# A metaformer block on one core: dot products through TensorE, one centring, sums per chunk, and other loop starts

## The reference, cut to what matters

```python
x = x + _L1_conv_ref(_ln_c(x), ...)      # _ln_c: (v - mean) / sqrt(var + 1e-6) over channels

center = x[:, :, H // 2, W // 2][:, :, None, None]
sim = (x * center).sum(1, keepdims=True) / (jnp.linalg.norm(center, axis=1, keepdims=True) * jnp.linalg.norm(x, axis=1, keepdims=True) + 1e-06)
x = x * (sim >= 0.7).astype(x.dtype)
xd = jnp.einsum('hH,bcHW,wW->bchw', Mh, x, Mw)
xt = xd.transpose(0, 2, 3, 1)
mu = xt.mean(-1, keepdims=True)
var = xt.var(-1, keepdims=True)
xn = ((xt - mu) / jnp.sqrt(var + 1e-05) * ln_w + ln_b).transpose(0, 3, 1, 2)
# four quadrants of xn each go through a mamba block (projection, short convolution, a scan
# of 16 states per channel over 1024 steps, gate, projection); xd + their outputs is
# transformed back
```

## Time and profile before

| | us |
|---|---|
| median of 3 runs | 4641.31 |
| lowest and highest run | 4617.7 and 4661.02 |
| the profiled execution | 4614.75 |
| its span | 4612.9 |

### The profile page before, as it was taken

The page is one execution under the profiler, slowest core; times in us unless marked ns, Lnnn a source line. Parts: engine busy times, 40 slices in busy tenths (PEclk is TensorE's granted clock), DMA queues, the critical chain, the costliest instruction groups (busy, mean ns, idle before and its releaser), DMA issues.

```text
span 4612.9 us, 49417 instructions
## 1 busy us (share of the span) xinstructions
PE 4009.5 (87%) x14248; PEld 1461.2 (32%) x14248; DVE 3563.9 (77%) x3093; ACT 2959.8 (64%) x3572; POOL 2483.7 (54%) x1148
## 2 busy tenths in 40 slices
PE   6779986899869998699986999779997799868997
PEld 2322233322332223322243222432233222332223
DVE  1469967699668996599965998659977699667996
ACT  2567756677566766577665675667757677565664
POOL 0237742577416873177731777227752477425774
PEclk9889998899989999799997999979999899987888
DMA  1147741577316763277623775347751577406661
GB/s 41 42 115 185 175 118 43 150 175 185 92 45 173 179 169 76 64 184 173 159 69 83 177 179 133 83 101 174 184 134 44 125 187 173 112 15 148 160 158 51
DMA packets 166836, 580.22 MB, mean 126 GB/s; under 512 B 22460, under 2 KB 23208, under 8 KB 162952
## 3 DMA queue, kind: packets, MB, share of 16 engines
q1 hardware_dynamic: 152168, 538.66, 47.6%
q10 hardware_dynamic: 14336, 37.76, 2.8%
HBM read 467.12 MB, written 71.48 MB: 117 GB/s over the span
## 4 chain that ended last, share of the span: by engine, by line
PE 56%; DVE 18%; issue 14%; ACT 8%; DMA 2%; POOL 1%; DVEq 0%; SPq 0%; ACTq 0%; POOLq 0%
PE ps L725 12%; PE ps L744 7%; PE ps L790 6%; DVE ps L1357 6%; PE ps L679 5%; DVE arena L1362 5%; PE ps L597 3%; PE ps L540 3%; PE ps L753 2%; PE ps L736 2%; PE ps L703 2%; PE ps L711 2%; ACT arena L887 2%; PE ps L695 2%; PE ps L687 2%
## 5 line engine op out<-in xcount | busy, mean ns | idle before, releaser
L1449 POOL TENSOR_TENSOR arena<-arena 128x1024 f32<-128x1024 f32 x768 | 1855.7, 2422 | 745.4 <-DVE arena L1362 744.8
L1362 DVE TENSOR_TENSOR_SCAN arena<-arena,ps 128x1024 f32<-128x1024 f32 x768 | 1756.1, 2287 | 98.4 <-ACT arena L1050 3.4
L1050 ACT ACTIVATE arena<-arena,a_all 128x1024 f32<-128x1024 f32 x768 | 873.0, 1141 | 340.7 <-DVE arena L1362 246.9
L1357 DVE TENSOR_TENSOR ps<-ps,arena 128x1024 f32<-128x1024 f32 x768 | 930.3, 1211 | 147.1 <-PE ps L727 146.2
L725 PE MATMUL ps<-arena,spread 32*128 32x512 f32 x1536 | 897.4, 672 | 96.7 <-DVE arena L1362 71.8
L727 PE MATMUL ps<-arena,spread 32*128 32x512 f32 x1536 | 883.6, 673 | 0.0
L744 PE MATMUL ps<-arena,gather 128*32 128x512 f32 x3072 | 536.4, 647 | 3.3 <-POOL arena L1449 2.3
L790 PE MATMUL ps<-x 96*96 96x512 f32 x1008 | 498.5, 612 | 0.0
L725 PEld LDWEIGHTS ps<-arena,spread 32*128 32x128 f32 x1536 | 233.0, 190 | 727.7 <-issue 420.2
L679 PE MATMUL ps<-arena,w_in 96*96 96x512 f32 x512 | 289.7, 718 | 37.0 <-DMA arena<-xq 37.0
L1403 POOL TENSOR_TENSOR x<-x,arena 96x512 f32<-96x512 f32 x64 | 113.9, 1780 | 369.1 <-DVE arena L1222 369.1
(11 more groups left out here) (160 smaller groups left out, 5758.2 us busy)
## 6 DMA issues: line engine op xcount, KB each, us to landing
arena<-dl SPq DMA_DIRECT2D x768, 512.0 KB, 5.3
dl<-arena ACTq DMA_DIRECT2D x64, 384.0 KB, 5.1
x<-pn SPq DMA_DIRECT2D x56, 247.5 KB, 5.0
arena<-in_x SPq DMA_DIRECT2D x9, 1536.0 KB, 14.7
arena<-xq SPq DMA_DIRECT2D x64, 192.0 KB, 6.1
arena<-arena ACTq DMA_DIRECT2D x64, 192.0 KB, 4.7
out<-x SPq DMA_DIRECT2D x64, 192.0 KB, 2.1
arena<-xq SPq DMA_DIRECT2D x64, 191.8 KB, 5.4
```

The lines of the kernel that those rows point to most:

```text
L1050: act.activation(da[:, m % DAS, :], dbc[:, m % DBC, :], ACT.Exp, scale=a_all[:, v // 2, m:m + 1]).then_inc(da_ready, 1)
L1357: dve.tensor_tensor(driven, driven, bmat[:, v % 2, :], ALU.mult).then_inc(bu_ready, 1)
L1362: dve.tensor_tensor_scan(hs[:, m % HSS, :], da[:, m % DAS, :], driven, 0.0, ALU.mult, ALU.add).then_inc(h_ready, 1)
L1449: pool.tensor_tensor(product, product, cmat[:, v % 2, :], ALU.mult).then_inc(pr_ready, 1)
```

## The change

- **Dot products by TensorE.** The moving matrix of the turning becomes `turn_by`, the centring matrix and two columns more. These hold the centred middle pixel, one image each, so each turned group of 98 columns ends with the two dot products. The middle pixel is fetched in `take_middle` by one matmul with two columns at the place of turn 0, and VectorE writes it into `turn_by` (`point_turn`). All eight turns are one step later. The spread of the middle pixel (L529) shrinks to its squared length. VectorE's and GpSimd's products go, and their sums. The turned data lie in a buffer `turned` of their own; the scaling writes `pix` from it.
- **Sums per chunk.** The squares are summed as each chunk arrives (`sum_squares`, 128x384 to 8), four inside the steps of the stream and four behind the last chunk sum.
- **One centring.** Channel means survive the mask and both transforms, so the second centring goes. ScalarE squares the row transform straight from PSUM behind each Copy; VectorE sums in halves, and each half has its own Ln and Exp.
- **Mask without reciprocal.** dot >= 0.7 * (lengths + 1e-6), as a comparison of two tensors, seven operations.
- **Loops.** VectorE's `pair` is cut into `both_norms` and `rest`, and the loop's body is `rest(p)`, `both_norms(p + 1)`: it turns over in front of the scans. ScalarE's is cut behind the roots. Both run six times, with the first and the last passes as code of their own. `router_max` stands between the two scalings, the router's exponential between the fourth and fifth column evacuation.

```diff
-        centre = sb("centre", [R, R])
+        turn_by = sb("turn_by", [R, R + 2])
+        centre = turn_by[:, 0:R]
+        of_image = sb("of_image", [R, 2])
...
+        TR = R + 2
+        MID = (H // 2) * W + W // 2
+        centre_ps = ps[:, 4, GB * TR:GB * TR + 2]
+        logits = ps[0:R, 6, GB * (R + 2):GB * (R + 2) + E]
...
+            def take_middle(P):
+                pe.wait_ge(hf_ready, P * 2 * NCH + NCH)
+                settled(pe)
+                pe.wait_ge(ffn_done, P * 2 * NCH + MID // CH + 1)
+                pe.matmul(ps[0:R, 4, 0:2], centre, x[:, MID:MID + 2], start=True, stop=True).then_inc(centre_row, 1)
...
-                    mm = pe.matmul(ps[:, 4 + n % 4, g * R:(g + 1) * R], x[:, px:px + 128], centre[:],
+                    mm = pe.matmul(ps[:, 4 + n % 4, g * TR:(g + 1) * TR], x[:, px:px + 128], turn_by[:],
                                    start=True, stop=True)
                 mm.then_inc(pix_ps, 1)
                 if n == 1:
                     pe.wait_ge(ln_act, P * LN_ACT + A_SQUARE)
-                    pe.matmul(centre_ps, sel_centre[:], pix[:, GRP // 2, :], start=True,
+                    pe.matmul(centre_ps, sel_centre[:], turned[:, GRP // 2, R:TR], start=True,
                               stop=True).then_inc(cen_ps, 1)
...
-                act.activation(chunk(pix, c), ps[:, 4 + n % 4, 0:GB * R], ACT.Copy).then_inc(pix_act, 1)
-                act.activation(chunk(pix2, c), ps[:, 4 + n % 4, 0:GB * R], ACT.Square).then_inc(ln_act, 1)
+                bank = ps[:, 4 + n % 4, 0:GB * TR]
+                act.activation(flat(turned)[:, c * GB * TR:(c + 1) * GB * TR], bank, ACT.Copy).then_inc(pix_act, 1)
+                act.activation(pix2[:, c * GB:(c + 1) * GB, :],
+                               bank.rearrange("p (g r) -> p g r", g=GB)[:, :, 0:R],
+                               ACT.Square).then_inc(ln_act, 1)
...
+                evac_turned(p, col, lambda c: ps_before(C_COL) + c + 1, range(NG // 2))
                 if not last:
                     router(p + 2)
-                evac_turned(p, col, lambda c: ps_before(C_COL) + c + 1)
+                evac_turned(p, col, lambda c: ps_before(C_COL) + c + 1, range(NG // 2, NG))
...
-                evac(p, C_ROW, flat(xd[:]), 128, 512)
+                for c in range(NCR):
+                    act.wait_ge(pix_ps, p * PS_PAIR + ps_before(C_ROW) + c + 1)
+                    part = slice(c * 512, (c + 1) * 512)
+                    act.activation(flat(xd[:])[:, part], ps[:, c, :], ACT.Copy).then_inc(pix_act, 1)
+                    act.activation(flat(pix)[:, part], ps[:, c, :], ACT.Square).then_inc(ln_act, 1)
                 for h in range(2):
-                    act.wait_ge(ln_dve, d0 + D_CENTRED2 + h)
-                    act.activation(halves(pix2)[h], halves(pix)[h], ACT.Square).then_inc(ln_act, 1)
-                act.wait_ge(ln_dve, d0 + D_VAR2)
-                act.activation(st[:, 2, :], st[:, 1, :], ACT.Ln, bias=eps[:, 1:2],
-                               scale=1.0 / C).then_inc(ln_act, 1)
-                act.wait_ge(ln_act, l0 + A_LOG2)
-                act.activation(st[:, 3, :], st[:, 2, :], ACT.Exp, scale=-0.5).then_inc(ln_act, 1)
+                    part = slice(h * (ST // 2), (h + 1) * (ST // 2))
+                    act.wait_ge(ln_dve, d0 + D_VAR2 + h)
+                    act.activation(st[:, 2, part], st[:, 1, part], ACT.Ln, bias=eps[:, 1:2],
+                                   scale=1.0 / C).then_inc(ln_act, 1)
+                    act.wait_ge(ln_act, l0 + A_LOG2 + 2 * h)
+                    act.activation(st[:, 3, part], st[:, 2, part], ACT.Exp, scale=-0.5).then_inc(ln_act, 1)
...
+            roots(0)
+            with act.Fori(0, PAIRS - 2) as p:
+                rest(p, False)
+                roots(p + 1)
+            rest(PAIRS - 2, False)
+            roots(PAIRS - 1)
+            rest(PAIRS - 1, True)
...
+                dve.tensor_copy(nrm[:, 0, ST:ST + 2], centre_ps).then_inc(centre_ready, 1)
+            def point_turn(P):
+                dve.wait_ge(centre_row, P + 1)
+                dve.tensor_tensor(turn_by[:, R:TR], ps[0:R, 4, 0:1].broadcast_to([R, 2]), of_image[:],
+                                  ALU.mult).then_inc(cvec_ready, 1)
+            def sum_squares(P, n):
+                c = IN_ORDER[n]
+                dve.wait_ge(ln_act, P * LN_ACT + A_SQUARE + n)
+                return dve.reduce_sum(nrm[:, 0, c * 2 * GB:(c + 1) * 2 * GB],
+                                      rows(pix2[:, c * GB:(c + 1) * GB, :]), AXX)
...
+                    n = turned_in(parts, t)
+                    if n == 0:
+                        take_middle(P)
+                    if n:
+                        turn_in(P, n - 1)
...
-                    if turned_in(parts, t) == 3:
+                    n = turned_in(parts, t)
+                    if n == 0:
+                        point_turn(P)
+                    if n and n >= 2:
+                        sum_squares(P, n - 2)
+                    if n == 4:
                         take_centre(P)
-                    if turned_in(parts, t) == 6:
-                        sum_first_half(P)
...
+                def scale(src, k, h):
+                    by_row = lambda t: half(t, h).rearrange("p g (i c) -> p g i c", c=C)
+                    dve.tensor_tensor(by_row(pix), by_row(src),
+                                      half_st(k, h).rearrange("p (g i o) -> p g i o", i=2, o=1)
+                                      .broadcast_to([128, GRP // 2, 2, C]), ALU.mult).then_inc(ln_dve, 1)
+                sum_squares(p, NG - 1).then_inc(ln_dve, 1)
                 if not last:
                     router_pool()
-                dve.wait_ge(ln_act, a0 + NG)
-                sums_of_squares(1).then_inc(ln_dve, 1)
-                dve.wait_ge(half_products, (p + 1) * (NG // 2))
-                link(dve.reduce_sum(half_st(4, 1), rows(half(xd, 1)), AXX))
-                if not last:
-                    router_max(p + 2)
+                dve.wait_ge(ln_act, a0 + A_RSTD)
+                link(dve.tensor_tensor(by_image(st[:, 0, :]), turned[:, :, R:TR], by_image(nrm[:, 2, 0:ST]),
+                                       ALU.mult))
+                link(dve.tensor_tensor(by_image(st[:, 1, :]), by_image(st[:, 0, :]),
+                                       of_centre(nrm[:, 2, ST:ST + 2]), ALU.mult))
                 dve.wait_ge(ln_act, a0 + A_ROOT)
                 link(dve.tensor_tensor(nrm[:, 5, :], nrm[:, 2, :], nrm[:, 4, :], ALU.mult))
                 link(dve.tensor_tensor(by_image(st[:, 5, :]), by_image(nrm[:, 5, 0:ST]),
                                        of_centre(nrm[:, 5, ST:ST + 2]), ALU.mult))
-                link(dve.tensor_scalar(st[:, 6, :], st[:, 5, :], 1e-6, None, ALU.add))
-                link(dve.reciprocal(st[:, 5, :], st[:, 6, :]))
-                link(dve.tensor_tensor(st[:, 0, :], st[:, 4, :], nrm[:, 2, 0:ST], ALU.mult))
-                link(dve.tensor_tensor(by_image(st[:, 1, :]), by_image(st[:, 0, :]),
-                                       of_centre(nrm[:, 2, ST:ST + 2]), ALU.mult))
-                link(dve.tensor_tensor(st[:, 6, :], st[:, 1, :], st[:, 5, :], ALU.mult))
-                link(dve.scalar_tensor_tensor(out=st[:, 7, :], in0=st[:, 6, :], scalar=0.7,
-                                              in1=nrm[:, 2, 0:ST], op0=ALU.is_ge, op1=ALU.mult))
-                for h in range(2):
-                    scale(7, h)
+                link(dve.tensor_scalar(st[:, 6, :], st[:, 5, :], 1e-6, 0.7, ALU.add, ALU.mult))
+                link(dve.tensor_tensor(st[:, 5, :], st[:, 1, :], st[:, 6, :], ALU.is_ge))
+                link(dve.tensor_tensor(st[:, 7, :], st[:, 5, :], nrm[:, 2, 0:ST], ALU.mult))
+                scale(turned[:, :, 0:R], 7, 0)
+                if not last:
+                    router_max(p + 2)
+                scale(turned[:, :, 0:R], 7, 1)
                 if not last:
                     dve.wait_ge(x_spilled, (p + 1) * 16)
                     router_choose(p + 2)
                 for h in range(2):
-                    dve.wait_ge(pix_act, p * ACT_PAIR + act_before(C_ROW) + (h + 1) * NCR // 2)
-                    subtract_mean(xd, h)
+                    dve.wait_ge(ln_act, a0 + A_SQUARE2 + (h + 1) * NCR // 2 - 1)
+                    dve.reduce_sum(half_st(1, h), rows(half(pix, h)), AXX).then_inc(ln_dve, 1)
                 for h in range(2):
-                    dve.wait_ge(ln_act, a0 + A_SQUARE2 + h)
-                    ins = dve.reduce_sum(half_st(1, h), rows(half(pix2, h)), AXX)
-                ins.then_inc(ln_dve, 1)
-                dve.wait_ge(ln_act, a0 + A_RSTD2)
-                for h in range(2):
-                    scale(3, h)
+                    dve.wait_ge(ln_act, a0 + A_LOG2 + 2 * h + 1)
+                    scale(xd[:], 3, h)
+                return steps[0]
+            def rest(p, last, linked):
+                base[0], steps[0] = p * CHAIN + 1 + PROLOGUE, linked
...
```

(10 more changed lines are left out.)

79 lines of the change are left out of this document (22 added, 57 removed).

## The result

| | before | changed |
|---|---|---|
| median us | 4630.19 | 4497.01 |
| lowest and highest of 4 runs | 4617.7 and 4661.02 | 4492.19 and 4507.71 |
| profiled execution, its span | 4614.75, 4612.9 | 4507.71, 4505.8 |

The ratio is 0.9706, with a 95% interval of 0.965 to 0.9762, so 110 to 162 us saved and 133 between the medians. The forecast was 130.5 us saved and 4511 us; the fourth run of the kernel before lowered that kernel's median from 4641 to 4630. The profiled execution of the changed kernel is its slowest of four, so the two profiles differ by 107 us only. I use both.

The account below looks back on a forecast made before the run. TensorE's waits in stretches A and B, mostly for VectorE, were taken to lie on the path once a pair. Savings of 81.6 and 48.9 us make 130.5, subtracted from the 4641.31 us median: 4511 us, range 4473 to 4557.

Parts of the forecast that it names:

- Stretch A: From VectorE's last chunk sum to TensorE's next transform, once a pair: 17.10 us to become 7.1, saving 77.6 us.
- Stretch B: From ScalarE's first row-transform evacuation to TensorE's next work: 15.62 us a pair to become 9.5, saving 48.9 us.
- The steps of the stream: Steps while the last chunks are normed: still 3.02 us, each new 0.55 us sum hidden in VectorE's 1.61 idle.
- The turn's old first place: One small matmul replaces the first turn, delaying TensorE's next average less: 0.5 us gained a pair, 4.0 in all.
- VectorE's gate choice: Moved behind the router's exponential, it waits some 4 us and takes 6, hidden before VectorE's next work 15 us away.
- The loop's turn-over: The 1.61 us gap in stretch A, 10.5 us over six pairs, goes when VectorE's loop turns over before the scans.
- Without that cover up to 1.8 us a pair would show: ScalarE's turn-over behind the roots, covered by some 4 us of small operations, first scaling and first transform chunk.
- the row over the page: Price of VectorE's turn-over: the profile row's 10.5 us for six, against 0.3 us in the run by the skill page.
- Rival 1: Costs of scalings, Copy and Square, first turn's answer and chunk sums at upper ends: 33 us less gain, 4544; chance 0.12.
- Rival 3: The wait moves: something else, such as the two spills, holds up the scans; no gain, 4641 us; chance 0.05.
- Rival 2: TensorE's clock stays at 2.4 GHz through the shorter gap into the transform: 14 us more saved, 4497 us; chance 0.10.
- Rival 4: Slower: TensorE falls to 1.2 GHz where it sets the pace, as in the scans; 4696 us with 23 us; chance 0.03.

Follow-up runs that it names:

- a_edges_back: The changed kernel with the loops of VectorE and ScalarE turned back to their old starts; 4539.28 us, ratio 0.982.
- b_edges_moved: The kernel before with only the loops' starts of VectorE and ScalarE moved as in the changed one; 4638.79 us, ratio 1.003.
- The busy kernels: The changed kernel with TensorE matmuls that nothing reads put into its pauses, in three extents; 4513.39, 4504.51 and 4513.46 us.
- a_busy_to_scans: The changed kernel with unread TensorE matmuls in the norms' pauses and between the turn back and the scans; 4504.51 us, ratio 0.9731.

## Why the prediction was right, step by step

- **Stretch A**: 7.1 us forecast, 7.14 measured; 76.5 us saved against 77.6. From the start of the last chunk sum, the forecast had the sums ended after 2.80 us, the roots back at 3.51, the first scaling at 5.30 and TensorE at 7.1. The rows have 2.73 (748.68), 3.45 (749.40), 5.32 (751.27) and 7.14 (753.09).
- **Stretch B**: 9.5 forecast, 9.49 measured in every pair; ScalarE's pitch was 0.48 for each Copy and Square, 0.96 for the pair against 0.98.
- **The steps of the stream** stayed at 3.02 us, with the sum in them and VectorE still idle for 1.15.
- **The turn's old first place**: the average starts 0.11 us behind the small matmul instead of 0.86, so 0.75 was gained there where I took 0.5. It comes through: from the first to the last of the eight chunk sums it is 22.93 us in every pair before (737.62 to 760.55 in pair 1) and 22.22 or 22.23 in every pair of the changed kernel's profile (723.73 to 745.95), with one step 3.45 us instead of 4.15 and the others equal. That is 5.7 us over eight pairs against the 4.0 of the sum. In the column of the way it can't be seen, as the inverse transforms, which did not change, take 0.5 to 1.8 us a pair more there (from the last scan to the first sum into `x` 26.4 to 27.7 us, against 25.9 before). No wait for `turn_by` appears.
- **VectorE's gate choice** waited 5.25 us (forecast 4) and cost nothing, as the scans begin at 802.06 behind 23.28 us of idle time.
- **The loop's turn-over is the step that was wrong, with a total that held.** The text put 10.5 us of stretch A's gain down to it and 67 to the work removed. By a_edges_back, the work removed brings 36.7 us of A as long as the turn-over stays where it was (133.3 to 96.6), and moving it 39.7 then; moving it alone brings 11.3 (b_edges_moved). VectorE's 6.1 us of products and sums were the cover of the turn-over: to take them out alone lays 6.33 us of it bare. The forecast came out right only because the change did both. "Without that cover up to 1.8 us a pair would show" for ScalarE was wrong by three times: 5.4 us a pair showed (12.5 against 7.1).
- The Trainium skill (Advanced Engine Details and Errata, Control Flow Timing) gives about 51 ns for a branch. The rows here show 6.33 us of issue on VectorE and 6.59 on ScalarE at a loop's turn-over. The measurement decides, and the choice of the row over the page was right in direction; even the row was a remainder.
- **Rival 1** fell: each cost lay at its nearer row. **Rival 3** fell: nothing in A or B waits for a transfer, and VectorE's start of the scans waits for ScalarE (23.28 us), not for a spill.
- **Rival 2** named 4497 us, and the median is 4497. Its mechanism is not why: the clock in A is 0.62 to 0.74, and in sum the transforms are not shorter. That the median falls on it is luck. My base was too high instead: with 4630, the median of four runs, the same sum gives 4500. The busy kernels show that its gain exists (14 to 16 us in the transforms) and that the scans take it back.
- **Rival 4**, slower through the clock, is partly real: not enough to decide here, but b_edges_moved is slower than before with A 11 us shorter. Its first units lost more to the late copy, a wait that neither the forecast nor a rival names, than to the clock directly.

What stays open is why a turn-over costs so much (the instruction packets are a hint), and what sets which first unit gets which clock. The rows show only which waits stand ahead of a fall. Open too, and cheap to try, is the order of the copy and the loads: issued ahead of them by design, it could spare up to 3.4 us wherever it now falls behind.

## What to carry to other kernels

An idle stretch put down to "issue" at a loop's edge is a remainder: add the work queued in front of it to get the price (here 7.7 to 7.9 us on VectorE, 6.6 on ScalarE), and put each engine's edge where it waits longer than that for something else before taking work out ahead of it. When runs of single parts don't add up, cut the profiles at the same rows: here B was worth 49.0 us each time while the runs said 41 and 76, and the difference lay in stretches that no edit touched. Within such a stretch, look at what ends TensorE's wait before putting it down to the clock: two queues that issue within 0.3 us of each other can change places, and a unit gets 3.4 us longer. Keeping TensorE fast ahead of a stage that another engine paces can cost its clock inside that stage, so count the whole pass, not the stretch.

## What the runs showed of the hardware that I had not expected

- A turn-over of a hardware loop: VectorE idle for 6.33 us behind 1.47 us of queued sums, ScalarE for 6.59 us behind nothing, TensorE for 1.54 us behind 2.8 us of queued matmuls (749.08 to 753.43 in a_busy_to_scans; put down to the turn-over by its place, not tested).
- The same work of a first unit took TensorE 29.97 us at a mean granted clock of 0.83 and 35.17 at 0.70, and the unit 34.8 and 40.1 us (pairs 2 and 1 of the changed kernel).
- A copy of 192 KB issued just ahead of four loads of 512 KB on another engine's queue landed after 2.4 to 3.1 us in 105 first units; issued 0.02 to 0.27 us behind the first of them, after 5.5 to 6.2 us in seven.
- Back to back from PSUM, ScalarE's activations of 128x512 show durations from 0.59 to 0.73 us while their pitch stays at 0.48. A price read from the duration would have been 20 to 50% too high.
